# Class rows' product before the third group's turnings, output biases on VectorE, and the first expert's parts inside the last batch

## The reference

```python
h = tok_ref(x, ...)                                   # (8, 256, 512)
h = concatenate([broadcast(cls_tok), h], axis=1)      # (8, 257, 512), row 0 is the class row
h = h + attn_ref(layernorm(h), Wq, bq, ..., Wo, bo, spiral_weight, helix_rotation)   # 16 heads of 32
# ffn_ref(layernorm(h)):
probs = softmax(x @ router_w + router_b)              # 8 experts
top_p, top_i = top_k(probs, 2); top_p = top_p / sum(top_p)
expert_out = gelu(einsum('bsh,ehd->ebsd', x, expert_w) + expert_b)
h = h + (sum over the two chosen experts of gate * expert_out) @ out_w + out_b
```

## Time and profile before

| What | Value |
| --- | --- |
| Time, median of 3 executions | 741.95 us (741.76 to 745.4) |
| The profiled execution, its own time | 743.96 us |
| Its span in the profile | 742.2 us |
| TensorE busy with matrix products | 677.8 us (91%) |
| VectorE busy | 525.4 us (71%) |
| ScalarE busy | 412.8 us (56%) |
| GpSimd busy | 152.6 us (21%) |
| Share of the chain that ended last: TensorE / VectorE / ScalarE | 72% / 17% / 4% |

### The profile page before, as it was taken

How to read it: one execution, slowest core, us unless ns; L and a number is a source line. 1 busy time by engine, 2 the same in 40 slices (tenths; PEclk the granted TensorE clock), 3 DMA queues, 4 the chain that set the end, 5 groups by cost and what they waited for, 6 DMA issues and landing times.

```text
span 742.2 us, 16679 instructions
## 1 busy us (share of the span) xinstructions
PE 677.8 (91%) x5671; PEld 541.1 (73%) x5672; DVE 525.4 (71%) x1210; ACT 412.8 (56%) x1073; POOL 152.6 (21%) x306
## 2 busy tenths in 40 slices
PE   4788977889999999999999999889679999998998
PEld 3577867767778787777878777656347888886886
DVE  7999883655788777787877877677884444445775
ACT  5864544486767677676766666665723333333111
POOL 5200001010121111201112020113132223336650
PEclk9889999979999999999999999999789999999999
DMA  7501255300000010000100003216626765556895
GB/s 202 198 1 29 115 143 145 73 1 1 3 29 30 0 56 0 29 28 14 42 0 28 28 28 115 85 58 227 256 60 207 206 202 162 167 168 204 263 325 172
DMA packets 54553, 76.11 MB, mean 103 GB/s; under 512 B 24666, under 2 KB 26970, under 8 KB 54387
## 3 DMA queue, kind: packets, MB, share of 16 engines
q1 hardware_dynamic: 40850, 42.43, 17.7%
q0 software_dynamic: 5920, 19.40, 9.9%
q10 hardware_dynamic: 7744, 13.77, 5.0%
HBM read 45.42 MB, written 30.16 MB: 102 GB/s over the span
## 4 chain that ended last, share of the span: by engine, by line
PE 72%; DVE 17%; ACT 4%; issue 3%; DMA 2%; POOL 1%; ACTq 0%; DVEq 0%; POOLq 0%; SPq 0%
PE ps L1978 45%; PE ps L2084 8%; PE ps L2094 4%; PE ps L2077 4%; PE ps L2145 3%; DVE ring L1409 3%; DVE ring L1408 3%; PE ps L1925 2%; PE ps L2101 1%; ACT prb L1029 1%; PE ps L1956 1%; ACT pts L1037 1%; DVE ew_lo L1720 1%; PE ps L1969 1%; PE ps L2044 1%
## 5 line engine op out<-in xcount | busy, mean ns | idle before, releaser
L1037 ACT ACTIVATE pts<-ps 128x512 f32<-128x512 f32 x128 | 77.0, 602 | 98.2 <-PE ps L2084 98.1
L1029 ACT ACTIVATE prb<-ps,negmax 128x257 f32<-128x257 f32 x256 | 117.7, 478 | 5.2 <-DVE negmax L1479 4.3
L1479 DVE TENSOR_REDUCE negmax<-ps 128x2 f32<-128x514 f32 x128 | 82.5, 686 | 22.4 <-PE ps L2077 22.4
L2084 PE MATMUL ps<-ident,prb 128*128 128x128 f32 x512 | 84.0, 287 | 5.7 <-ACT pts L1037 3.2
L2084 PEld LDWEIGHTS ps<-ident,prb 128*128 128x128 f32 x512 | 57.1, 143 | 30.8 <-issue 13.1
L1488 DVE TENSOR_SCALAR prb<-prb,rrec 128x258 f32<-128x258 f32 x256 | 73.5, 351 | 2.3
L1211 ACT ACTIVATE rows<-ps 128x512 f32<-128x512 f32 x40 | 23.9, 598 | 87.5 <-DVE ps L1835 85.5
L1978 PE MATMUL ps<-ew_hi,xnT_hi 128*128 x160 | 66.7, 417 | 3.0 <-DVE xnT_lo L1756 2.4
L1978 PE MATMUL ps<-ew_lo,xnT_hi 128*128 x160 | 63.5, 397 | 0.0
L1978 PE MATMUL ps<-ew_hi,xnT_lo 128*128 x160 | 63.0, 394 | 0.0
L839 POOL DMA_INDIRECT rows<-xn_dram,token_of x40 | 39.6, 990 | 106.9 <-PE ps L2145 87.1
(11 more groups left out here) (402 smaller groups left out, 1761.1 us busy)
## 6 DMA issues: line engine op xcount, KB each, us to landing
y_slots<-rows ACTq DMA_DIRECT2D x40, 256.0 KB
ew<-in_L_ffn_expert_w_dram SPq DMA_DIRECT2D x8, 1024.0 KB, 9.1
h_dram<-h_ob SPq DMA_DIRECT2D x17, 256.0 KB, 2.0
xn_dram<-tok SPq DMA_DIRECT2D x17, 256.0 KB, 2.2
h_late<-h_dram SPq DMA_DIRECT2D x12, 256.0 KB
out_dram<-h_late SPq DMA_DIRECT2D x11, 256.0 KB
y_slots<-u_sb SPq DMA_DIRECT2D x9, 256.0 KB, 5.4
tok_dram<-so SPq DMA_DIRECT2D x4, 512.0 KB, 3.1
```

What stands on the lines that cost most here:

```text
L1029: e = act.activation(prb[:, u % 2, j, 0:KEYS], ps[:, j, 0:KEYS], ACT.Exp, bias=negmax[:, u % 2, j:j + 1], accum_out=rowsum[:, u % 2, j:j + 1])
L1037: act.activation(pts[:, slot:slot + 2, :, st * P:(st + 1) * P], ps[:, 4, :].rearrange("p (h t s) -> p h t s", h=2, t=HALVES), ACT.Copy).th ...
L1479: dve.tensor_reduce(negmax[:, u % 2, 2 * b:2 * b + 2], ps[:, 2 * b:2 * b + 2, 0:KEYS], AX_X, ALU.max, negate=True).then_inc(s["dve_max"], 1)
L2084: mm = pe.transpose(ps[:, 4, (2 * j + tt) * P:(2 * j + tt + 1) * P], prb[:, u % 2, 2 * b + j, tt * P:(tt + 1) * P], ident[:, :])
```

## The change

Six edits, all in the written order of the engines' programs.

1. TensorE: the class rows' product stands ahead of the turnings of the third group.
2. The last output bias additions (last batch's two tiles, and the class tile) move from GpSimd to VectorE (`out_bias`). The one for the first tile takes the place of half an expert's low part, the second stands ahead of the last norms, the class tile's stands behind `rsc`.
3. The first expert's high part moves into unit 3 of the last batch on ScalarE, and its low part in two halves into units 4 and 5 on VectorE, each ahead of `residual_stats`.
4. The second expert's low part is made in halves: ahead of the class rows' residual, and behind the third group's `top_two`.
5. Behind the routing: the gates' three operations move ahead of the wait for `pe_token_of`; the three for `stores_used` and the low part of expert 5 move behind the first two `lo_xs`.
6. Memory: `reached` is placed earlier and a piece of 280 words is left free, so that the first expert's high part lies on memory that the last batch no longer reads.

```diff
@@ ScalarE, unit 3 of the last batch
                     if u == 3 and last:
                         keep_xnT(1)
+                        act.wait_ge(s["pe_values"], NB * HALVES)
+                        hi_expert(0)
@@ ScalarE, behind the last batch
             hi_ot(last, 3)
-            hi_expert(0)
             hi_expert(1)
@@ GpSimd, behind the last batch
             last = NB - 1
-            for st in range(HALVES):
-                pool.wait_ge(s["dve_residual"], 2 * last + st + 1)
-                pool.wait_ge(st_h[st], 16 * NB)
-                add_bias(last, st)
             norm_pow(last)
             pool.wait_ge(s["dve_stats2"], 5 * NB + 3)
             pool.tensor_tensor(rsc[:, 1, :], rsc[:, 0, :], mhalf[:, :], ALU.pow).then_inc(s["pool_rstd"], 1)
-            pool.wait_ge(st_h[0], 16 * (NB + 1))
-            pool.tensor_tensor(h_ob[:, 0, :], tok[:, CLS, :], ob[:, :], ALU.add).then_inc(s["pool_out_bias"], 1)
@@ VectorE, the last batch's after_norm
+                    if u == 4 and last:
+                        lo_chunks(0, 0, KC // 2)
+                    if u == 5 and last:
+                        lo_chunks(0, KC // 2, KC).then_inc(s["dve_expert_low"], 1)
                     if u == 5 and not last:
                         lo_qk(c + 1, 0)
                     if not first:
@@ VectorE, the end of attention
+            def out_bias(st, t):
+                dve.wait_ge(st_h[st], 16 * NB if t != CLS else 16 * (NB + 1))
+                dve.tensor_tensor(h_ob[:, st, :], tok[:, t, :], ob[:, :], ALU.add).then_inc(s["out_bias_added"], 1)
 
             top_two(1)
             residual(last, 0, 6)
             dve.wait_ge(s["dve_residual"], last * HALVES + 1)
             residual_stats(last, 0)
-            lo_chunks(0, 0, KC // 2)
+            out_bias(0, last)
             residual(last, 1, 7)
             dve.wait_ge(s["dve_residual"], last * HALVES + 2)
             residual_stats(last, 1)
             dve.wait_ge(s["dve_stats2"], 5 * last + 2)
             norm_sums(last)
-            lo_chunks(0, KC // 2, KC).then_inc(s["dve_expert_low"], 1)
+            out_bias(1, NB + last)
             for st in range(HALVES):
                 normalise(last, st)
+            lo_chunks(1, 0, KC // 2)
             dve.wait_ge(s["loaded_cls"], 16)
             dve.wait_ge(s["pe_cls_projected"], 1)
...
-            lo_expert(1)
+            out_bias(0, CLS)
             dve.wait_ge(s["pool_rstd"], NB + 1)
-            dve.wait_ge(s["pool_out_bias"], NT)
+            dve.wait_ge(s["out_bias_added"], NT)
...
                 top_two(q - 1)
+                if q == EARLY_QUADS + 1:
+                    lo_chunks(1, KC // 2, KC).then_inc(s["dve_expert_low"], 1)
@@ VectorE, behind the routing
             lo_expert(2)
             lo_chunks(LOWS_IN_ATTENTION + 1, KC // 2, KC)
-            lo_chunks(LOWS_IN_ATTENTION + 2, 0, KC)
...
             lo_xs(0, 0)
             lo_xs(1, 1)
+            then(dve.tensor_scalar(pairs_used[:, 0:1], tiles_to[:, 1, 3 + NE:4 + NE], 0.5, 0.25, ALU.mult, ALU.add))
+            then(dve.tensor_scalar(pairs_used[:, 1:2], pairs_used[:, 0:1], ROUND_MAGIC, ROUND_MAGIC, ALU.add, ALU.subtract))
+            dve.tensor_scalar(stores_used[:, :], pairs_used[:, 1:2], 16.0, None, ALU.mult).then_inc(s["dve_stores_used"], 1)
+            lo_chunks(LOWS_IN_ATTENTION + 2, 0, KC)
@@ TensorE, the end of attention
             project(last, 1, 7)
-            for n in range(4 * EARLY_QUADS, 4 * EARLY_QUADS + 4):
-                turn_xn(n)
             pe.wait_ge(s["dve_spread"], 18)
...
             mm.then_inc(s["pe_cls_projected"], 1)
+            for n in range(4 * EARLY_QUADS, 4 * EARLY_QUADS + 4):
+                turn_xn(n)
             logits_of(EARLY_QUADS)
```

More of the change, by code:

```diff
@@ L222, in vit_tower_kernel @@
         xhat = sb(at, "xhat", [P, HALVES, D])
+        sb(at, "rest_of_first_high", [P, 280])
         q_hi = sb(at, "q_hi", [P, KC, KPAD], F32R)
@@ L284, in vit_tower_kernel @@
         eb = sb(ffn, "eb", [P, NE, D])
+        reached = sb(ffn, "reached", [P, SLOTS, NE - 1])
         gates = sb(ffn, "gates", [P, NT, SEL])
@@ L331, in vit_tower_kernel @@
             "pool_rstd": "the second norm's 1 / sqrt for a batch",
-            "pool_out_bias": "a tile with the output bias added, to be kept for the end",
+            "out_bias_added": "a tile with the output bias added, to be kept for the end",
             "pool_sums_cleared": "zeros ahead of the tiles' sums, then where the running sums of an expert begin",
@@ L596, in _ @@
                 keep_xn(NB - 1, st)
-            sp.wait_ge(s["pool_out_bias"], NT)
+            sp.wait_ge(s["out_bias_added"], NT)
             sp.dma_start(h_dram[CLS], h_ob[:, 0, :]).then_inc(st_h[0], 16)
@@ L1067, in keep_lgT, with hi_expert @@
                 act.activation(dst[:, 0:w], ps[:, bank, 0:w], ACT.Copy).then_inc(s["act_logitsT_kept"], 1)
+            def hi_expert(e):
+                act.wait_ge(ld_ew[e], ew_from[e] + 16)
+                act.activation(ew_hi[:, e, :, :], ew[:, e, :, :], ACT.Copy).then_inc(s["act_expert_high"], 1)
             def body(c, first, last):
@@ L1511, in normalise @@
             def normalise(m, st):
[L1512 removed]
+                dve.wait_ge(s["out_bias_added"], 2 * m + st + 1)
                 dve.wait_ge(s["pool_rstd"], m + 1)
@@ L1561, in top_two, with lo_chunks, lo_expert @@
                 then(e)
+            def lo_chunks(e, k0, k1):
+                dve.wait_ge(s["act_expert_high"], e + 1)
+                return dve.tensor_tensor(ew_lo[:, e, k0:k1, :], ew[:, e, k0:k1, :], ew_hi[:, e, k0:k1, :].bitcast(F32),
+                                         ALU.subtract)
+            def lo_expert(e, done=1):
+                lo_chunks(e, 0, KC).then_inc(s["dve_expert_low"], done)
             def before_norm(c, u, first, last):
@@ L1717, in _ @@
                               ).then_inc(s["dve_spread"], 1)
-            def lo_chunks(e, k0, k1):
-                dve.wait_ge(s["act_expert_high"], e + 1)
-                return dve.tensor_tensor(ew_lo[:, e, k0:k1, :], ew[:, e, k0:k1, :], ew_hi[:, e, k0:k1, :].bitcast(F32),
-                                         ALU.subtract)
-            def lo_expert(e, done=1):
-                lo_chunks(e, 0, KC).then_inc(s["dve_expert_low"], done)
+            def out_bias(st, t):
+                dve.wait_ge(st_h[st], 16 * NB if t != CLS else 16 * (NB + 1))
+                dve.tensor_tensor(h_ob[:, st, :], tok[:, t, :], ob[:, :], ALU.add).then_inc(s["out_bias_added"], 1)
             top_two(1)
@@ L1804, in _ @@
                                   bc(slot_place[:, c0:c1].unsqueeze(2), shape), ALU.is_equal).then_inc(s["dve_onehot"], 1)
+            dve.wait_ge(s["act_route_exp"], 1)
+            then(dve.tensor_scalar(spread[:, 2, :], spread[:, 1, :], 1.0, None, ALU.add))
+            then(dve.reciprocal(gates[:, :, 0], spread[:, 2, :]))
+            dve.tensor_tensor(gates[:, :, 1], gates[:, :, 0], spread[:, 1, :], ALU.mult).then_inc(s["dve_gates"], 1)
             dve.wait_ge(s["pe_token_of"], 1)
@@ L1815, in _ @@
             dve.tensor_copy(expert_of[:, :], tile_expert[:, :]).then_inc(s["dve_expert_of"], 1)
-            then(dve.tensor_scalar(pairs_used[:, 0:1], tiles_to[:, 1, 3 + NE:4 + NE], 0.5, 0.25, ALU.mult, ALU.add))
-            then(dve.tensor_scalar(pairs_used[:, 1:2], pairs_used[:, 0:1], ROUND_MAGIC, ROUND_MAGIC, ALU.add, ALU.subtract))
-            dve.tensor_scalar(stores_used[:, :], pairs_used[:, 1:2], 16.0, None, ALU.mult).then_inc(s["dve_stores_used"], 1)
-            dve.wait_ge(s["act_route_exp"], 1)
-            then(dve.tensor_scalar(spread[:, 2, :], spread[:, 1, :], 1.0, None, ALU.add))
-            then(dve.reciprocal(gates[:, :, 0], spread[:, 2, :]))
-            dve.tensor_tensor(gates[:, :, 1], gates[:, :, 0], spread[:, 1, :], ALU.mult).then_inc(s["dve_gates"], 1)
             lo_expert(2)
             lo_chunks(LOWS_IN_ATTENTION + 1, KC // 2, KC)
-            lo_chunks(LOWS_IN_ATTENTION + 2, 0, KC)
             def lo_xs(i, u):
```

9 lines of the change are left out of this document (2 added, 7 removed).

## The result

The changed kernel takes 747.49 us (median of 21 executions, 742.83 to 752.41), the kernel before 741.47 beside it on the same chip (21 executions, 737.0 to 745.4). The ratio is 1.0075, 95% interval 1.0059 to 1.0091. The profiled execution of the changed kernel took 748.41 with a span of 746.7; the mean clock granted to TensorE was 0.968 in it, as in the profiled one of before.

The account below looks back on a forecast made before the run. TensorE, busy 91% of the span, was taken as the bound, losing only where it waits for another engine. Terms 1.2 + 0.1 + 1.8 + 1.6 = 4.7 us on the median 741.95 gave 746.6, 0.6% slower; range 743.0 to 749.0.

Parts of the forecast that it names:

- Term 1: Last batch: high part and unit 4's half free, unit 5's half delays the maxima and `pv`; +1.2 us.
- I take the whole 1.2 as lost: Last batch, unit 5: all later matrix work queues behind `pv`, so the half's 1.2 us is lost in full.
- one more slow stretch, in unit 6 of the last batch: Rival: TensorE's pause before `pv` grows by 1.2, bringing another half-clock stretch; 1.7 us more, 748.3; chance 0.13.
- a stretch falls soon behind it anyway and may only move: Last batch: argument against the extra 1.7 us, as a half-clock stretch already follows soon behind TensorE's pause before `pv`.
- Term 2: End of attention: the stall only goes from VectorE and GpSimd to ScalarE; +0.1 us, bounds -0.5 and +0.4.
- the lower bound: End of attention: -0.5 us, if TensorE's slow stretch (half clock) at 523 no longer falls there.
- Term 3: Start of expert loop: held gather and three whole low parts delay bias addition 0 and product 2; +1.8 us.
- The hold of the gather: Expert loop's start: gather begun during VectorE's subtraction gets on when that ends, then needs 0.9; tile 1's is 1.3 late.
- as I had read from expert 5's part: Expert loop's start: expert 5's low part took 2.29 as any other, though a gather was under way until 546.87.
- it stays: Expert loop: from product 2 on TensorE is the bound again, so the +1.8 us delay remains.
- Term 4: TensorE's clock: half-speed stretch behind the new 2.9 us pause before product 2; +1.6 us, bounds 0 and 1.8.
- I expect a slow stretch behind it: Expert loop: half clock follows the 2.9 us pause before product 2, on work nothing covers, priced at 1.6 us.

Follow-up runs that it names:

- first_in_batch: Kernel before with only the first expert's high part in unit 3 and low part in units 4 and 5 of the last batch; 745.4 us, ratio 1.005.
- the four and the five traces above: Four kernels with the old loop-start order, five with all three late low parts; product 2 starts 16.91 to 17.92 and 18.09 to 19.15 us behind the slot table.
- loop_start_only: Kernel before with only the routing's tail reordered (gates, stores, low parts of experts 2 and 5); 742.69 us, ratio 1.0012.

## Why the prediction was right, and where it was not

The forecast of 746.6 and "0.6% slower" stands beside 1.0075, on 741.47. The mechanism of each wait was right; that the total is, is partly luck: term 1 is too small by 2.5 us and terms 3 and 4 together too large by as much, and the two errors cancel.

- **Term 1, +1.2.** The wait came as worked out: 1.14 us at `pv(1)`, unit 4's half and the high part free. As the price of the part it is too small by a factor of about three: first_in_batch measured 3.7. The mis-sized step is "I take the whole 1.2 as lost": it counts the wait and not what TensorE's clock does behind it. That was there as a rival ("one more slow stretch, in unit 6 of the last batch", 0.13), set aside because "a stretch falls soon behind it anyway and may only move". It did not only move: the trace of the change has three lengths of it for one, and those of two others have two.
- **Term 2, +0.1** (bounds -0.5 to +0.4). The trace says -0.45, the ratio 1.0003. The stall went from VectorE and GpSimd to ScalarE's copies, as described, but the class tile was turned without any wait, and the slow stretch at 523 was gone: the reason I had given for the lower bound.
- **Term 3, +1.8.** In the trace 2.21 at product 2, with bias addition 0 late by 2.70 (the prediction's 556.6 for 553.86 says 2.7). The prediction had set its 559.2 against 557.36, where the chain puts product 2; the timeline's row of its first instruction is at 557.12, and by that the term would have been 2.1. By the means of the four and the five traces above product 2 is 1.4 late. The hold of the gather is shown by its length of 2.30, and by 1.30 when the subtraction was cut in four. The Trainium skill, page "SBUF — State Buffer", section "SBUF: two separate sides", says that a VectorE instruction with two inputs from SBUF and a GpSimd operation that reads SBUF exclude each other for the whole instruction, whichever starts first. By that expert 2's low part would also have had to wait for gather 0. It began at 545.31 while that gather lay from 544.43 to 545.82, and the row of the whole and the half low part took 3.42, no more than such parts take elsewhere (2.29 and 1.21). So the trace shows the hold in one direction only, as I had read from expert 5's part. What the term brought over the whole kernel is less: 0.9 in loop_start_only, together with term 4, by an interval that reaches to 2.7. Where no slow stretch comes, some 0.5 us of it is left at bias addition 4, so "it stays" held only in part.
- **Term 4, +1.6.** This is the failed step, "I expect a slow stretch behind it". It came in three traces of five, not always, and not in the change's. Where it came it was dear, some 2 us at bias addition 4, but on average it is worth less than the full 1.6, and loop_start_only leaves no room for terms 3 and 4 at full size, 3.4 us.

What stays open: why slow stretches follow the pause of 2 us in some executions and not in others; how often the kernel before has one there, as its one trace does; and what TensorE of the kernel before waits for ahead of its product 4.

## What to carry to other kernels

Where TensorE carries the chain, price a pause twice: the wait itself, and what the clock does behind it. Here 1.15 us of VectorE's time in one unit cost 3.7 to 4.4. An "idle" slot on another engine is only free if it ends before somebody waits: unit 4's slot had 1.32 us of idle time for 1.22 of work, unit 5's had none. Several executions are needed to see it, since a single trace may show none of the slow stretches or all. A long subtraction on VectorE should not start just ahead of a gather of GpSimd that something waits for: cut into four pieces it held the gather 1.0 us less.

## What the runs showed of the hardware that was not expected

- Idle time can cost more than work that nobody needs: with twelve added turnings of 128x128, 1.3 us of TensorE, the ratio was 1.0049 for 1.0075 (the intervals overlap).
- Kernels that are equal up to the last batch show their slow stretches at different times in their traces even there, and a kernel's executions differ by up to 10 us: in the 21 of the change the mean clock goes from 0.963 (752.41 us) to 0.977 (745.5), at some 0.5 us for each thousandth.
- The class rows' power on GpSimd takes 1.06 us where VectorE's bias addition of 0.68 runs beside it, and 2.66 beside a low part of 2.29.
